# One issuing queue for all transfers of a fused attention and feed-forward kernel, in a new order

## The chip, the core and the metric

The kernel runs on one core of a Trainium2 chip. A core has a matrix engine (TensorE, PE in the rows), three engines for elementwise work (VectorE or DVE, ScalarE or ACT, GpSimd or POOL), and SyncE (SP), which here only issues transfers. Each engine works through its own list of instructions in order and waits on semaphores. Transfers (DMA) are issued from an engine's queue (SPq, ACTq) and carried out by 16 shared DMA engines. Time is device microseconds of one launch.

## What is computed

Eight batches of 128 tokens, 512 wide, go through one gated cross-attention and one gated feed-forward block, in float32:

```python
x = x + jnp.tanh(g_xattn[0]) * xattn(_layernorm(x), ctx, ctx, Wq, bq, Wk, bk, Wv, bv, Wo, bo)
x = x + jnp.tanh(g_ffn[0]) * ffn(_layernorm(x), w1, w1_scale, w3, w3_scale, w2, w2_scale)
# xattn: 32 query heads of 16 over 8 key heads, softmax(Q K^T / 4) V, then Wo
# ffn: silu(x W1^T) * (x W3^T), then W2^T; 1792 inner columns, weights scaled by 128 x 128 blocks
```

## The kernel before

**Precision.** Most products are made from a high and a low piece of each operand (three matmuls, lines 1871 to 1873): names that end in H and L, or PH and PL for the softmax numerators.

**Attention, batch by batch.** A pair of batches shares a projection of Q (four `project_q`), K and V (`project_kv32`). K and Q go out to DRAM scratch (kscr, qscr) and come back in another layout: `keys_out`, six strips of 64 KB by `keys_in` into x2HL (whose memory holds the keys until the feed-forward needs it), `queries_out`, three blocks by `queries_in` (or `queries_part` for batch 0) into Qst. `scores(n, j)` (line 1917) makes scores only for their row maxima: VectorE reduces them (MX, Mtok), TensorE turns them (`turn_max`), they become Mrow and come back as one more strip of Qst (`max_in`). `scores_t(n, g)` (line 1928) then makes the transposed scores with the maxima subtracted by that strip, together with a fixed pattern `sel` that stands as rows in x2HL (`select_rows`). ScalarE takes the exponential twice (E and PH), GpSimd makes PL = E - PH (line 460), `values(n, g)` multiplies with V (lines 1936, 1937), VectorE divides (on), and after a turn (`turn4`), aTH and aTL, `project` with the output weights WpH, WpL gives the residual (line 1279). Then the second norm: statistics, x2n, a turn, and x2H (ScalarE) and x2L (VectorE) in x2HL.

**Feed-forward.** 14 chunks of 128 inner columns in two halves of four batches. A chunk's weights arrive in wres (`weights_in`, 768 KB), GpSimd scales them (`scale`, line 471), ScalarE and VectorE split them (w13H, w13L, w2H, w2L), TensorE makes `g_or_u` and `y`. The first three chunks start among the last attention work. The first `y` waits for the last x2L, since its four banks of PSUM are those of the attention work.

**What sets the order.** Everything is one straight program per engine, written out by hand up to the loop of the feed-forward. Transfers are issued by SyncE (lines 266 to 411) and, for 22 of them, by ScalarE between its compute instructions. Buffers with few slots tie the engines together: E and PL have four slots, Qst three, the keys four batches.

The lines on which most turns: the third part of the first queries and what waits for it,

```python
            queries_part(sp, 0, 0, 0, 2, q_in1a)      # SyncE, line 297
            out_weights_in(sp)                        # 1 MB, line 298
            queries_part(act, 0, 1, 0, 2, q_in1a)     # ScalarE, line 830
            pe.wait_ge(q_in1a, 48)                    # TensorE, ahead of scores(0, 0)
```

Of the kernel before, what the change touches and what calls it, by code (L numbers as in the profile page):

```python
# [66 lines left out]
def build(nc, x, ctxt, wproj, bias, small, wff, out):  # L67
    with ExitStack() as ctx:
# [3 lines left out]
        def sem(name):  # L72
            return ctx.enter_context(nc.semaphore(name))
# [101 lines left out]
        mean2_ok, ve2_ok, rs2_ok, nb2_ok, x2n_ok, x2T_ps = (sem(n) for n in ("mean2_ok", "ve2_ok", "rs2_ok", "nb2_ok", "x2n_ok", "x2T_ps"))
        x2H_ok, x2L_ok, q_in2, q_in0, nb2_ok_pool, x2n_ok_dve = (sem(n) for n in ("x2H_ok", "x2L_ok", "q_in2", "q_in0", "nb2_ok_pool", "x2n_ok_dve"))
        scaled, w13H_ok, w13L_ok, g_ps, u_ps, t_ok = (sem(n) for n in ("scaled", "w13H_ok", "w13L_ok", "g_ps", "u_ps", "t_ok"))
        a_ok, h_ok, hH_ok, w2H_ok, w2L_ok, hL_ok = (sem(n) for n in ("a_ok", "h_ok", "hH_ok", "w2H_ok", "w2L_ok", "hL_ok"))
        y_used, warmed = sem("y_used"), sem("warmed")
# [17 lines left out]
        def select_rows(eng, b):  # L197
            done = (sel_in0, sel_in1, sel_in2, sel_in3)[b]
            eng.dma_start(r32(kst(b)[ROWS:ROWS + NM, :, :]), sel[ROWS:ROWS + NM, :, :]).then_inc(done, 16)
# [67 lines left out]
        def _(sp):  # L267
# [6 lines left out]
            for b in (2, 3):  # L274
                tokens_in(sp, b)
                context_in(sp, b)

            sp.wait_ge(kh_out, 16)
            keys_in(sp, 0, 2, 1)
            keys_in(sp, 0, 0, 1)  # L280
            sp.wait_ge(kl_out, 16)
            keys_in(sp, 0, 1, 1)
            sp.wait_ge(qT_H, 2)
            queries_out(sp, 0, 0, 0, 2, qh_outa)
            keys_in(sp, 0, 1, 0)
            keys_in(sp, 0, 2, 0)
            tokens_in(sp, 5)
            sp.wait_ge(kT_H_dve, 1)
            keys_out(sp, 1, 0)
            sp.wait_ge(kT_L, 2)  # L290
            keys_out(sp, 1, 1)
# [6 lines left out]
            out_weights_in(sp)  # L298
            sp.wait_ge(kh_out, 32)
            keys_in(sp, 1, 0, 1)  # L300
            tokens_in(sp, 6)
# [3 lines left out]
            queries_part(sp, 0, 2, 2, 4, q_in1)  # L305
            sp.wait_ge(kT_L, 3)
            keys_out(sp, 2, 1)
            keys_out(sp, 2, 0)
            keys_in(sp, 1, 1, 0)
            queries_in(sp, 1, 2, q_in2)  # L310
            queries_in(sp, 1, 0, q_in2)
            context_in(sp, 6)
            keys_in(sp, 1, 2, 1)
            context_in(sp, 7)
            sp.wait_ge(sel_ok, 3)
            select_rows(sp, 3)
            sp.wait_ge(mrows, 1)
            max_in(sp, 0, 0, 2)
            sp.wait_ge(qT_H, 8)
            queries_out(sp, 1, 0, 0, 4, qh_out)  # L320
            sp.wait_ge(qT_L, 8)
            queries_out(sp, 1, 1, 0, 4, ql_out)
            sp.wait_ge(qh_out, 32)
            queries_in(sp, 2, 0, q_in0)
            sp.wait_ge(ql_out, 32)
            queries_in(sp, 2, 2, q_in0)
            keys_in(sp, 1, 2, 0)
            keys_in(sp, 1, 1, 1)
            sp.wait_ge(kT_H_dve, 3)
            keys_out(sp, 3, 0)  # L330
            select_rows(sp, 1)
# [2254 lines left out]
```

## Time and profile before

| | before |
|---|---|
| median of 3 runs | 393.6 us (390.91 to 394.44) |
| the profiled execution | 394.24 us |
| its span in the trace | 392.5 us |
| TensorE busy | 369.7 us, 94% of the span |
| VectorE, ScalarE, GpSimd busy | 259.1, 182.3, 152.8 us |
| mean granted clock of TensorE | 0.982 of full speed |
| DMA | 34.96 MB, 89 GB/s over the span |

The profile is of one execution. A row of a timeline has a start, a duration and, in brackets, how long the engine was idle ahead of it and which instruction or transfer ended that. The time of an instruction that is blocked while it holds its engine is in its duration, not in the brackets.

### The profile page before, as it was taken

Reading aid. Unit: us, or ns where it says so; the run is one execution under the profiler, and the core shown is the slowest. Engines: PE = TensorE matmul, PEld = TensorE weight load, DVE = VectorE, ACT = ScalarE, POOL = GpSimd, SP = SyncE. Lnnn points to the kernel's source line nnn. Section 1 sums busy time; section 2 is a strip of 40 time slices with the busy share of each in tenths; the row PEclk is TensorE's granted clock in tenths of the full one; section 3 lists DMA queues with packets and bytes.
Section 4 is the critical chain, followed back from the end, with each engine's and each line's share of the span. In section 5 each row is a group of like instructions: output and inputs, shape, how many; then the busy total and the mean of one; then the engine's idle time right before and its main releaser. Section 6 shows DMA issues by size and latency. Waiting matters only on the chain.

```text
span 392.5 us, 6021 instructions
## 1 busy us (share of the span) xinstructions
PE 369.7 (94%) x2216; PEld 303.0 (77%) x2216; DVE 259.1 (66%) x417; ACT 182.3 (46%) x316; POOL 152.8 (39%) x134
## 2 busy tenths in 40 slices
PE   8977699979999999879999999999999999999996
PEld 6967589868677878658888888888888888888885
DVE  4764869969999967876776777543855344544334
ACT  3442579858889985243233242232242232332320
POOL 5463558979999987442333344000000000000000
PEclk9996989999999999989999999999999999999999
DMA  8899545936861310691000000000200000000002
GB/s 302 267 320 238 182 100 112 243 85 205 199 163 28 104 71 2 249 424 51 0 0 0 0 0 0 0 0 0 109 1 0 0 0 0 0 0 0 0 0 107
DMA packets 15604, 34.96 MB, mean 89 GB/s; under 512 B 2176, under 2 KB 7296, under 8 KB 14784
## 3 DMA queue, kind: packets, MB, share of 16 engines
q1 hardware_dynamic: 12080, 28.84, 24.0%
q10 hardware_dynamic: 3504, 5.86, 5.3%
q8 instruction: 12, 0.20, 0.2%
q14 instruction: 8, 0.07, 0.1%
HBM read 26.04 MB, written 7.34 MB: 85 GB/s over the span
## 4 chain that ended last, share of the span: by engine, by line
PE 55%; DVE 1%; issue 0%
PE ps L1871 19%; PE ps L1873 18%; PE ps L1872 18%; DVE X L1306 1%; DVE hL L1328 0%
## 5 line engine op out<-in xcount | busy, mean ns | idle before, releaser
L1871 PE MATMUL ps<-x2HL,w13H 128*128 128x512 f32 x224 | 89.0, 397 | 0.0
L1873 PE MATMUL ps<-x2HL,w13L 128*128 128x512 f32 x224 | 88.5, 395 | 0.0
L1872 PE MATMUL ps<-x2HL,w13H 128*128 128x512 f32 x224 | 88.4, 395 | 0.0
L460 POOL TENSOR_TENSOR PL<-E,PH 128x512 f16<-128x512 f32 x64 | 74.1, 1177 | 12.3 <-ACT PH L753 4.8
L471 POOL TENSOR_TENSOR wres<-wres,gsc 128x1536 f32<-128x1536 f32 x14 | 41.8, 2989 | 49.3 <-DVE hf L1319 49.3
L772 ACT ACTIVATE T<-ps 128x512 f32<-128x512 f32 x28 | 16.7, 597 | 79.4 <-PE ps L1873 79.4
L1873 PEld LDWEIGHTS ps<-x2HL,w13L 128*128 128x128 f32 x224 | 42.0, 187 | 10.4
L1872 PEld LDWEIGHTS ps<-x2HL,w13H 128*128 128x128 f32 x224 | 42.0, 188 | 10.0
L1871 PEld LDWEIGHTS ps<-x2HL,w13H 128*128 128x128 f32 x224 | 42.0, 188 | 9.6
L1312 DVE SCALAR_TENSOR_TENSOR A<-T,ps 128x512 f32<-128x512 f32 x28 | 19.2, 686 | 45.4 <-ACT T L772 45.4
L1871 PE MATMUL ps<-w2H,hH 128*128 128x512 f32 x112 | 45.1, 403 | 2.3 <-DVE x2HL L1295 2.3
L1248 DVE TENSOR_REDUCE MX<-ps 128x8 f32<-128x1024 f32 x32 | 38.9, 1217 | 12.5 <-PE ps L1917 12.1
L780 ACT ACTIVATE hH<-hf 128x512 fp32r<-128x512 f32 x28 | 17.7, 631 | 62.9 <-DVE hf L1319 62.9
L1873 PE MATMUL ps<-w2H,hL 128*128 128x512 f32 x112 | 44.3, 395 | 0.0
L1872 PE MATMUL ps<-w2L,hH 128*128 128x512 f32 x112 | 44.1, 394 | 0.0
L1319 DVE SCALAR_TENSOR_TENSOR hf<-A,ps 128x512 f32<-128x512 f32 x28 | 19.2, 687 | 32.4 <-PE ps L1873 32.1
L753 ACT ACTIVATE PH<-ps 128x512 f16<-128x512 f32 x64 | 37.2, 599 | 6.9 <-PE ps L1928 6.9
L1328 DVE TENSOR_TENSOR hL<-hf,hH 128x512 fp32r<-128x512 f32 x28 | 38.3, 1369 | 2.4
L750 ACT ACTIVATE E<-ps 128x512 f32<-128x512 f32 x64 | 37.4, 598 | 3.8 <-PE ps L1928 3.7
L1300 DVE TENSOR_TENSOR w13L<-wres,w13H 128x1024 fp32r<-128x1024 f32 x28 | 34.1, 1219 | 5.4 <-ACT w13H L767 5.4
L1928 PE MATMUL ps<-Qst,x2HL 112*128 112x512 f32 x64 | 27.5, 445 | 3.5 <-DMA Qst<-Mrow 3.5
L1917 PE MATMUL ps<-x2HL,Qst 96*128 96x256 f32 x128 | 22.6, 302 | 8.3 <-DMA Qst<-qscr 4.4
(103 smaller groups left out, 651.7 us busy)
## 6 DMA issues: line engine op xcount, KB each, us to landing
wres<-in_wff SPq DMA_DIRECT2D x12, 768.0 KB, 7.7
Qst<-qscr SPq DMA_DIRECT2D x19, 256.0 KB, 4.5
X<-in_x SPq DMA_DIRECT2D x6, 256.0 KB, 6.0
qscr<-QTH SPq DMA_DIRECT2D x3, 512.0 KB, 2.9
qscr<-QTL SPq DMA_DIRECT2D x3, 512.0 KB, 4.9
wres<-in_wff ACTq DMA_DIRECT2D x2, 768.0 KB, 7.0
out<-X SPq DMA_DIRECT2D x6, 256.0 KB, 2.1
x2HL<-kscr SPq DMA_DIRECT2D x20, 64.0 KB, 4.3
```

The lines of the kernel that those rows point to most:

```text
L460: pool.tensor_tensor(PL[:, g % NL, :], E[:, g % NE, :], PH[:, g, :], ALU.subtract).then_inc(pL_ok, 1)
L471: pool.tensor_tensor(w, w, v, ALU.mult).then_inc(scaled, 1)
L750: act.activation(E[:, g % NE, :], ps[:, g % 2, :], ACT.Exp, scale=SCALE).then_inc(E_ok, 1)
L753: act.activation(PH[:, g, :], ps[:, g % 2, :], ACT.Exp, scale=SCALE).then_inc(PH_ok, 1)
L1248: dve.tensor_reduce(MX[:, j, :, :], ps[:, b:b + 2, :].rearrange("p b (x g k) -> p (b x) g k", x=2, g=2), AX.X, ALU.max).then_inc(max_ok, 1)
L1300: dve.tensor_tensor(w13L[:, s, :], wres[:, n, 0:W13], r32(w13H[:, s, :]), ALU.subtract).then_inc(w13L_ok, 1)
L1328: dve.tensor_tensor(hL[:, s, :], hf[:, s, :], r32(hH[:, s, :]), ALU.subtract).then_inc(hL_ok, 1)
L1871: pe.matmul(out_ap, aH, bH, start=start, stop=False)
L1872: pe.matmul(out_ap, aH, bL, start=False, stop=False)
L1873: return pe.matmul(out_ap, aL, bH, start=False, stop=stop)
L1917: m = pe.matmul(ps[:, b + h // 2, (h % 2) * TWO:(h % 2 + 1) * TWO], Qst[0:ROWS, slot(n), h, j * P:(j + 1) * P], kst(n)[0:ROWS, 2 * h:2 * h ...
L1928: pe.matmul(ps[:, g % 2, :], kst(n)[0:ROWS + NM, g, :], Qst[0:ROWS + NM, slot(n), g // 2, :], start=True, stop=True).then_inc(st_ps, 1)
```

## The change

- All 22 transfers that ScalarE issued during the attention go to SyncE; ScalarE keeps its first three. SyncE's list goes from 98 to 120 transfers, in a new order: the 1 MB of output weights behind all parts of the first queries and two blocks of the next, tokens and context 6 and 7 behind those, feed-forward chunks 0 and 1 behind a group of keys and queries.
- The select pattern is made on GpSimd first of all and its four strips go out right after the first ten loads, under one semaphore.
- x2n is made on ScalarE for all eight batches (VectorE made the last one). ScalarE also takes the bias copies of V (VT) and three of K (KTH) from VectorE, VectorE takes a max strip and its low half.
- The interleaving of all engines' lists is written anew around that. The instructions of TensorE are the same, but one V projection stands earlier and one K projection later than the first scores, and two thirds of an output projection move behind the last `values`.

```diff
@@ SyncE, from the first wait on
+            sp.wait_ge(sel_ok, 3)
+            for b in range(NKST):
+                select_rows(sp, b)
+            sp.wait_ge(kT_H, 1)
+            keys_out(sp, 0, 0)
+            sp.wait_ge(kT_L, 1)
+            keys_out(sp, 0, 1)
+            sp.wait_ge(v_ps, 1)
+            context_in(sp, 4)
+            context_in(sp, 5)
+            tokens_in(sp, 4)
...
             queries_part(sp, 0, 0, 0, 2, q_in1a)
-            out_weights_in(sp)
+            queries_part(sp, 0, 1, 0, 2, q_in1a)
+            sp.wait_ge(ql_outa, 16)
+            queries_part(sp, 0, 2, 0, 2, q_in1a)
...
             queries_in(sp, 1, 0, q_in2)
+            out_weights_in(sp)
+            queries_in(sp, 1, 1, q_in2)
             context_in(sp, 6)
...
@@ VectorE
-            def normalise2(n):
-                dve.tensor_scalar(x2n[:], X[:, n, :], rs2[:, n % 2, 0:1], nb2[:, n % 2, 0:1], ALU.mult, ALU.add).then_inc(x2n_ok_dve, 1)
```

**Place 1: SyncE, from the second half of the first queries out to the first max strip.** qscr is the scratch for queries, Qst<-qscr the way back, raw<-in_wproj the output weights, x2HL<-kscr a strip of keys. Before:

```order
L223 DMA qscr<-QTL 128x2x256
L231 DMA Qst<-qscr 32x4x256
L205 DMA raw<-in_wproj 128x2048
L219 DMA x2HL<-kscr 16x4x256
L202 DMA X<-in_x 128x512
L231 DMA Qst<-qscr 32x4x256 x2
L214 DMA kscr<-KTL 128x256
L214 DMA kscr<-KTH 128x256
L219 DMA x2HL<-kscr 16x4x256
L227 DMA Qst<-qscr 32x2048 x2
```

and after the change:

```order
L221 DMA qscr<-QTL 128x2x256
L229 DMA Qst<-qscr 32x4x256 x3
L212 DMA kscr<-KTH 128x256
L229 DMA Qst<-qscr 32x4x256 x3
L225 DMA Qst<-qscr 32x2048 x2
L203 DMA raw<-in_wproj 128x2048
L225 DMA Qst<-qscr 32x2048
L240 DMA ct<-in_ctxt 128x512
L200 DMA X<-in_x 128x512
L240 DMA ct<-in_ctxt 128x512
L200 DMA X<-in_x 128x512
```

All six parts of batch 0 and two blocks of batch 1 now stand ahead of the output weights; three of the parts were ScalarE's before.

**Place 2: SyncE, the strips and blocks of the fifth batch (its third pair).** Before, with the first chunk of feed-forward weights (wres) issued by ScalarE meanwhile:

```order
L235 DMA Qst<-Mrow 16x4x512
L219 DMA x2HL<-kscr 16x4x256 x2
L227 DMA Qst<-qscr 32x2048 x3
L219 DMA x2HL<-kscr 16x4x256 x3
L235 DMA Qst<-Mrow 16x4x512
```

and after:

```order
L233 DMA Qst<-Mrow 16x4x512
L217 DMA x2HL<-kscr 16x4x256 x3
L225 DMA Qst<-qscr 32x2048
L217 DMA x2HL<-kscr 16x4x256 x2
L225 DMA Qst<-qscr 32x2048 x2
L217 DMA x2HL<-kscr 16x4x256
L237 DMA wres<-in_wff 128x1536
```

The chunk of weights now follows all nine transfers on the same queue.

**Place 3: VectorE, the end of the attention.** hf is the gated product of the feed-forward, the x2HL rows are the low pieces of the second norm. Before:

```order
L1319 SCALAR_TENSOR_TENSOR hf<-A,ps 128x512
L1252 TENSOR_SCALAR x2n<-X,rs,nb 128x512
L1324 TENSOR_TENSOR w2L<-wres,w2H 128x512
L1295 TENSOR_TENSOR x2HL<-ps,x2HL 128x4x128 x2
L1328 TENSOR_TENSOR hL<-hf,hH 128x512
L1324 TENSOR_TENSOR w2L<-wres,w2H 128x512
```

and after:

```order
L1306 TENSOR_TENSOR x2HL<-ps,x2HL 128x4x128
L1335 TENSOR_TENSOR w2L<-wres,w2H 128x512
L1330 SCALAR_TENSOR_TENSOR hf<-A,ps 128x512
L1306 TENSOR_TENSOR x2HL<-ps,x2HL 128x4x128
L1339 TENSOR_TENSOR hL<-hf,hH 128x512
L1335 TENSOR_TENSOR w2L<-wres,w2H 128x512
L1306 TENSOR_TENSOR x2HL<-ps,x2HL 128x4x128
L1339 TENSOR_TENSOR hL<-hf,hH 128x512
```

x2n is gone from VectorE, and the last x2HL has two w2L and an hL ahead of it.

## Rows read from the trace of the kernel before

**Rows 1.** The page: busy time and share of the span by engine.
```profile
PE 369.7 (94%) x2216; PEld 303.0 (77%) x2216; DVE 259.1 (66%) x417; ACT 182.3 (46%) x316; POOL 152.8 (39%) x134
```
**Rows 2.** Windows: from:to, length, then busy by engine, clock, DMA share, GB/s.
```profile
0.00:27.70 27.70, 25.37 (x138) 22.00 (x138) 17.78 (x43) 11.92 (x20) 14.75 (x21) 1.00 0.91 300
27.70:49.20 21.50, 13.65 (x89) 12.93 (x89) 12.66 (x21) 7.93 (x13) 10.17 (x10) 0.84 0.83 211
49.20:60.00 10.80, 10.80 (x86) 9.56 (x87) 7.64 (x17) 8.07 (x17) 6.52 (x7) 0.84 0.41 95
60.00:82.60 22.60, 19.75 (x213) 17.45 (x211) 19.96 (x41) 19.64 (x40) 21.17 (x24) 1.00 0.72 183
82.60:150.90 68.30, 65.93 (x682) 52.46 (x683) 58.24 (x132) 57.48 (x111) 61.73 (x58) 1.00 0.42 113
150.90:170.20 19.30, 15.19 (x83) 11.97 (x79) 17.76 (x27) 9.30 (x15) 10.61 (x7) 1.00 0.51 202
170.20:177.40 7.20, 7.20 (x25) 5.85 (x26) 4.89 (x7) 2.10 (x3) 2.76 (x1) 0.76 1.01 420
177.40:392.50 215.10, 211.83 (x913) 170.81 (x911) 120.18 (x133) 65.80 (x98) 25.11 (x8) 1.00 0.03 11
```
**Rows 3.** Timeline of TensorE: start, duration, and the idle before it.
```profile
27.40 0.28 PE L1873 MATMUL ps<-xTH,WpL 128*128 128x256 f32 x1
32.11 2.05 PE L1917 MATMUL ps<-x2HL,Qst 96*128 96x256 f32 x8 [4.43 <-DMA Qst<-qscr]
...
49.18 0.73 PE L1928 MATMUL ps<-Qst,x2HL 112*128 112x512 f32 x2 [3.18 <-DMA Qst<-Mrow]
...
82.61 0.73 PE L1917 MATMUL ps<-x2HL,Qst 96*128 96x256 f32 x4 [2.85 <-DMA x2HL<-kscr]
...
150.90 0.18 PE L1937 MATMUL ps<-Vp,PL 128*128 128x49 bf16 x1
...
165.82 0.66 PE L1879 MATMUL ps<-ident,x2n 128*128 128x128 f32 x4 [1.81 <-DVE x2n L1252]
...
170.18 0.80 PE L1871 MATMUL ps<-w2H,hH 128*128 128x512 f32 x1 [2.30 <-DVE x2HL L1295]
```
**Rows 4.** DMA issues around 22.5 us: what, size, us from issue to landing.
```profile
raw<-in_wproj SPq DMA_DIRECT2D x1, 1024.0 KB, 9.0
Qst<-qscr ACTq DMA_DIRECT2D x1, 128.0 KB, 9.7
```
**Rows 5.** Windows 17.3 to 40.8 and 1.5 to 12.5.
```profile
17.30:40.80 23.50, 18.28 (x116) 17.02 (x115) 13.92 (x30) 9.49 (x16) 9.85 (x12) 0.85 0.97 263
...
1.50:12.50 11.00, 10.99 (x46) 9.10 (x47) 6.21 (x15) 5.58 (x8) 7.15 (x8) 1.00 0.99 357
```
**Rows 6.** DMA issues around 42.9 us: the second max strip.
```profile
Qst<-Mrow ACTq DMA_DIRECT2D x1, 64.0 KB, 6.5
```
**Rows 7.** ScalarE's timeline at 74; DMA issues around 76.4 us.
```profile
74.44 0.35 ACTq L239 DMA_DIRECT2D wres<-in_wff  x1
...
x2HL<-kscr SPq DMA_DIRECT2D x1, 64.0 KB, 6.8
```
**Rows 8.** Windows around the wait at 82.6.
```profile
70.00:82.60 12.60, 9.76 (x100) 8.24 (x98) 10.12 (x21) 9.64 (x19) 12.11 (x13) 1.00 0.81 205
82.60:90.00 7.40, 7.39 (x93) 6.72 (x94) 6.04 (x11) 4.58 (x10) 4.97 (x3) 1.00 0.30 61
```
**Rows 9.** The tail: timelines of VectorE and GpSimd; groups of w2L and of ScalarE's x2n.
```profile
162.81 2.96 DVE L1252 TENSOR_SCALAR x2n<-X,rs,nb 128x512 f32<-128x512 f32 x1 [0.43 <-POOL nb L450]
165.69 3.24 DVE L1324 TENSOR_TENSOR w2L<-wres,w2H 128x512 fp32r<-128x512 f32 x1
...
162.73 5.65 POOL L471 TENSOR_TENSOR wres<-wres,gsc 128x1536 f32<-128x1536 f32 x2
...
L1324 DVE TENSOR_TENSOR w2L<-wres,w2H x28: 679/684/3240, 165.7 to 384.4; 128x512 fp32r<-128x512 f32 x28
...
L728 ACT ACTIVATE x2n<-X,nb,rs x7: 805/827/880, 104.7 to 158.6; 128x512 f32<-128x512 f32 x7
```

More of the change, by code:

```diff
@@ L846, in _ @@
+            q_high(W2, 2)
+            act.wait_ge(q_ps, 4)
+            q_high(W1, 3)
             act.wait_ge(r1_ok, 2)
             v_second(2, W0)
+            act.wait_ge(k_ps, 2)
+            act.wait_ge(kh_out, 16)
+            act.wait_ge(kl_out, 16)
+            k_high(W2)
+            act.wait_ge(xT_ps, 3)
+            normalise(3)
+            x_high(2, W1)
+            gates()
+            act.wait_ge(v_ps, 3)
+            v_bias(W0)
+            act.wait_ge(xT_ps, 4)
+            x_high(3, W2)
@@ L1386, in _ @@
[L1386 to L1391 removed]
+            dve.wait_ge(stats1, 4)
+            mean(3)
+            dve.wait_ge(qT_H, 3)
+            q_low(W2, 2)
+            dve.wait_ge(mean1, 4)
+            epsilon(3)
+            v_residue(2, W0)
+            dve.wait_ge(rs1_ok, 4)
+            shift(3)
+            dve.wait_ge(qT_H, 4)
+            q_low(W1, 3)
+            dve.wait_ge(v2_ok_act, 2)
@@ L2227, in _ @@
             scores_t(3, 0)
+            pe.wait_ge(max_ok, 18)
+            scores(4, 2)
+            pe.wait_ge(PH_ok, 24)
+            scores_t(3, 1)
             pe.wait_ge(pL_ok, 21)
@@ L2447, in _ @@
             values(6, 4)
+            project(W1, DM, aTH, aTL, O0, 3, True).then_inc(o_ps, 1)
+            pe.wait_ge(PH_ok, 56)
+            scores_t(7, 1)
+            pe.wait_ge(PH_ok, 57)
+            scores_t(7, 2)
             pe.wait_ge(pL_ok, 54)
             values(6, 5)
-            pe.wait_ge(E_ok, 56)
-            scores_t(7, 1)
-            g_or_u(0, 0, 0, 0, range(2, KB))
+            pe.wait_ge(w13L_ok, 1)
+            g_or_u(0, 0, 0, 0, range(2))
+            pe.wait_ge(E_ok, 58)
+            scores_t(7, 3)
             pe.wait_ge(pL_ok, 55)
@@ L2487, in _ @@
             values(7, 4)
-            project(W1, DM, aTH, aTL, O0, 2)
             pe.wait_ge(pL_ok, 62)
             values(7, 5)
-            project(W1, DM, aTH, aTL, O0, 3, True).then_inc(o_ps, 1)
-            pe.wait_ge(E_ok, 63)
-            pe.wait_ge(w13L_ok, 2)
-            g_or_u(1, 1, 0, 0, range(2))
+            pe.wait_ge(x2n_ok, 5)
+            turn4(W0, x2n).then_inc(x2T_ps, 1)
+            pe.wait_ge(aTL_ok, 7)
+            project(W2, DM, aTH, aTL, O0, 0)
+            project(W2, DM, aTH, aTL, O0, 1)
             pe.wait_ge(pL_ok, 63)
```

1619 lines of the change are left out of this document (778 added, 841 removed).

## The prediction

> **What bounds the kernel now.** Start with the busy line of the page [rows 1]: TensorE is busy for 369.7 us, 94% of the span, and the next engine for 66%. So only three things can pay: TensorE's idle time (22.8 us in all), the stretches in which it ran at the lower of its two clock levels (1.2 instead of 2.4 GHz; the mean granted clock of a window tells the share), and work taken off it. The change takes no matmul away: both programs issue the same matmuls, in another order. The windows by stage [rows 2] show where the loss sits: 0 to 49.2 us holds 10.2 us of idle (2.3 + 7.9) and clock 0.84 in its second part; 49.2 to 60 is busy all through at clock 0.84; 60 to 150.9 holds 5.2 us; 150.9 to 170.2 holds 4.1, and the 7.2 us after it run at clock 0.76; from 177.4 on nothing is left but 3.3 us at the end. The waits on TensorE's own timeline [rows 3] name them: 4.43 us for Qst<-qscr before the first scores, 3.18 for the max rows before the first transposed scores (which I call ST), 2.85 for keys at 82.6, 1.81 for a normalised row block (x2n) that VectorE made, and 2.30 for x2HL before the first product with w2.
>
> **Part 1, the way to the first scores.** Scores(0,0) starts at 32.11, when the third part of the queries lands: ScalarE had issued it 9.7 us before it landed, and 1 MB of output weights, issued on SyncE's queue half a microsecond earlier, took 9.0 us beside it [rows 4]. TensorE had run dry at 27.68 [rows 3]. The change sends these parts before the 1 MB. I count the bytes that the one queue carries from the end of the first ten loads (about 12.5 us, with the DMA engines 99% busy until then [rows 5]) to that third part: four select strips 256 KB, first keys out 256, three blocks of tokens or context 768, six key strips 384, tokens 5 256, gates 85, bias 256, queries out 1024, three parts 384. Together 3669 KB, or 3.76 MB. In 17.3 to 40.8 us the DMA engines were 97% busy and moved 263 GB/s [rows 5]: 14.3 us, so 26.8. TensorE's own work ahead of it shrinks by one key projection (1.7 us), but its second query product now waits for the third V split: by the durations of ScalarE and VectorE I place it at 27.3. Scores(0,0) at 27.3 instead of 32.1.
>
> **Part 2, from there to the first ST.** Before, this took 17.1 us (32.11 to 49.18): the second max strip needed 6.5 us on ScalarE's queue, beside 1 MB of queries out on SyncE's [rows 6], so it was issued at 42.7. TensorE has exactly the same matmuls behind it at this point in both programs (three K, four V, eight query products, six score groups), so the two times compare directly. After: from the third part to the second max strip the queue carries keys out 128 KB, parts 384, queries of batch 1 768, output weights 1024, four input blocks 1024, keys 64, strip 64, keys out 128, queries out 512, strip 64: 4160 KB, 4.26 MB. All at 263 GB/s gives 16.2 us and 43.0; the 2.1 MB of wide loads at the 357 GB/s of the first loads [rows 5] and the rest at 263 gives 14.1 and 40.9. TensorE's own work reaches ST at about 41. I take 42.0 for ST, bounds 41 and 43 (45 if the V chain slips as well): gain 7.2 us, bounds 4 to 8.
>
> **Part 3, the clock behind it.** The 10.8 us from 49.2 to 60 ran at 0.84 after the 3.18 us wait: 10.8 x 0.16 = 1.7 us. The wait before ST should now be under 1 us, and after the 2.85 us wait at 82.6 the clock stayed at 1.00 [rows 3, 8]. I take the 1.7 whole; the other bound is 0.
>
> **Part 4, keys for the fifth batch.** The last of six key strips took 6.8 us to land, next to 768 KB of feed-forward weights that ScalarE had sent at 74.44 [rows 7]. Now the weights go out after all keys and queries. Those nine transfers take 384 + 768 KB, 1.18 MB, 4.5 us at 263 GB/s against issues of some 6 us, and ten us of matmuls stand between their release and their use, so the 2.85 us wait should go. But GpSimd was busy for 12.1 of the 12.6 us around it and for 5.0 of the 7.4 after it [rows 8]; it was behind and used the wait. I take half, 1.4 us, bounds 0 and 2.85. ScalarE is rid of 22 issues (0.35 us for the one in [rows 7], longer for strips) and takes seven K and V copies; busy for 57.5 of 68.3 us and 19.6 of 22.6 [rows 2] it has the room, so I put nothing down.
>
> **Part 5, the tail.** From the last value matmuls (150.90) to the first w2 product (170.18) are 19.3 us [rows 3]. VectorE's x2n took 2.96 us and w2L after it 3.24 (median 0.68), both while GpSimd ran two weight scalings in 5.65 us; ScalarE makes an x2n in 0.83 [rows 9]. So x2n goes to ScalarE and its 1.81 us wait goes. But w2L, h and w2L again now stand on VectorE ahead of the last x2L (the second order piece), for which the w2 product waits, and GpSimd's scalings are released in the same microseconds as before. Walking the queues with those durations (on 2.1 us, o_ps 7.8, x2n ready 11.5, w2L 13.9, second hf 14.6, h 17.9, w2L 18.5, x2L 19.1) gives 19.1 us, 18.3 where VectorE gets ahead of the first scaling. In addition 1.0 us of matmuls moved behind the start of this stretch. Gain 1.0 + 0.2 to 1.0; I take 1.3. The lower clock after it (0.76 for 7.2 us) I leave as it is. If nothing were blocked, x2L would be ready at 15.1 and TensorE would not wait: 3.3 us more, and 1.7 of clock.
> The Trainium skill, SBUF — State Buffer, section SBUF: two separate sides, says that VectorE and GpSimd share one port pair as an exclusive lock: whoever starts first holds it for its whole instruction, also against a VectorE instruction with two SBUF inputs. The trace agrees (2.96 and 3.24 us). By it moving x2n alone does not free the tail, which is what I forecast; without it the sum would be some 5 us lower.
>
> **The sum.** 7.2 + 1.7 + 1.4 + 1.3 = 11.6 us. The profiled execution took 394.24 us (span 392.5 [rows 1] and 1.7 around it), the median of the three runs is 393.6; the gain is in waits that every run has, so I take it from the median: 382.0.
>
> **Rivals.**
> Given back (22%): ST comes 7 us sooner, but the dense middle is held by GpSimd (61.7 of 68.3 us busy, 21.2 of 22.6 before that [rows 2]) and by ScalarE, and a strip that is now queued behind 1 MB of queries out (the fifth batch's) comes late. Then parts 3 and 4 bring nothing and two waits like the old 2.85 come in: 393.6 - 7.2 - 1.3 + 2 to 7 us, 387 to 392.
> Slower (10%): one queue moves less than two. The strip must be there by 49.2, so 6549 KB between 17.3 and 49.2: below 210 GB/s part 2 turns into a loss, and below some 180 GB/s (38 us, ST at 55) it eats everything else: 396 or more. For it: 60 to 82.6 moved only 183 GB/s [rows 2]. Against it: the DMA engines were 72% busy there, and the first loads, nearly all on SyncE's queue, made 357.
> The Trainium skill, DMA: Bandwidth & Descriptors, section Issuing engines are not separate DMA queues, says that transfers of all queues run on the same 16 engines and that issuing from several saves only issue time; by it this rival falls away. ScalarE's own queue did not let the 64 KB strip past in this trace (6.5 us), which agrees.
> More (12%): the tail is unblocked too, 382.0 - 5 = 377 or less.
> My own case 56%, 378 to 387.
>
> **Numbers.** A difference of under about 1% cannot be told from no change here (390.91 to 394.44 in three runs). Faster by over 1% is below 389.7: 56 + 12 + 14 of the 22 = 82%. Within 1%: 8 + 3 = 11%. Slower: 7%. The range 376 to 390 leaves out some 2 in 10: the slower rival, the end of "given back", and the far end of "more".
>
> **What would show it.** Right: scores(0,0) at 26 to 29 us; ST at 40 to 44 with a wait under 1.5; clock 1.00 from 30 to 60; no wait for kscr near 74; no VectorE x2n; w2L still near 3 us beside a scaling, and some 3 us of wait for x2HL before the first w2 product. Wrong: DMA busy at 97% with far less than 263 GB/s; waits for Mrow strips or keys that the trace of before does not have; GpSimd with no idle from 45 to 140 while TensorE waits for PL.

## The result, and the profile after

The changed kernel takes 390.48 us (median of 20 runs, 386.82 to 395.74), the kernel before 393.6 us (20 runs, 390.07 to 396.92). The ratio is 0.992, with a 95% interval of 0.989 to 0.995: 3.1 us less, small but clear of the noise over 20 runs, and under the 1% that the prediction could not tell from no change. Predicted were 382.0 us, 376 to 390. Of the 11.6 us forecast, 8.5 did not come. A second profile of the changed kernel, taken later, reads like the first (391.55 us); the first is shown here.

TensorE's share on the page has grown by one point, in a span that is 3.2 us shorter:

```profile
span 389.3 us, 6031 instructions
...
PE 371.2 (95%) x2216; PEld 303.8 (78%) x2216; DVE 253.6 (65%) x411; ACT 184.7 (47%) x322; POOL 154.9 (40%) x134
```

Windows of the changed kernel (columns as in [rows 2]: length; busy time of PE, PEld, DVE, ACT, POOL; granted clock, DMA share, GB/s):

```profile
0.00:27.70 27.70, 24.35 (x131) 20.68 (x132) 15.90 (x40) 14.18 (x26) 13.98 (x22) 1.00 0.85 260
27.70:49.20 21.50, 16.38 (x93) 14.96 (x91) 10.65 (x18) 6.53 (x10) 10.70 (x8) 0.76 0.91 251
49.20:60.00 10.80, 10.80 (x100) 9.82 (x99) 9.40 (x21) 9.69 (x20) 7.48 (x9) 1.00 0.56 110
```

Its TensorE timeline, the places that answer to [rows 3] (start, duration, idle before it and its releaser); L1912 are scores, L1925 transposed scores, L1893 K and V projections (x4 or x8 is the number of matmuls in a row):

```profile
29.82 1.40 PE L1912 MATMUL ps<-x2HL,Qst 96*128 96x256 f32 x8 [1.75 <-DMA Qst<-qscr]
42.02 1.19 PE L1912 MATMUL ps<-x2HL,Qst 96*128 96x256 f32 x4 [3.38 <-DMA Qst<-qscr]
43.22 2.02 PE L1893 MATMUL ps<-ct,raw 128*128 128x256 f32 x4
...
49.42 1.03 PE L1893 MATMUL ps<-ct,raw 128*128 128x256 f32 x4
50.09 0.59 PE L1925 MATMUL ps<-Qst,x2HL 112*128 112x512 f32 x1
...
80.40 0.73 PE L1912 MATMUL ps<-x2HL,Qst 96*128 96x256 f32 x4 [1.07 <-DMA x2HL<-kscr]
105.97 0.62 PE L1912 MATMUL ps<-x2HL,Qst 96*128 96x256 f32 x3 [1.62 <-DMA x2HL<-kscr]
148.13 0.18 PE L1934 MATMUL ps<-Vp,PL 128*128 128x49 bf16 x1
166.94 0.64 PE L1866 MATMUL ps<-w2H,hH 128*128 128x512 f32 x1 [2.74 <-DVE x2HL L1306]
```

Set against [rows 3], these rows divide the 3.2 us of span among the stages:

| stage | before | after | gain | predicted |
|---|---|---|---|---|
| start to first transposed scores (ST) | 49.18 | 50.09 | -0.9 | 7.2 |
| ST to last value product | 101.7 | 98.0 | 3.7 | 4.1 (parts 3 and 4, and the 1.0 of part 5 that moves behind this stage) |
| last value product to first w2 product | 19.3 | 18.8 | 0.5 | 0.3 (the rest of part 5) |
| first w2 product to end of span | 222.3 | 222.4 | -0.1 | 0 |

So everything behind ST went about as forecast, and the whole miss is ahead of it. Scores(0,0) came at 29.8 instead of 27.3. Then a wait appeared that the prediction had nowhere: 3.38 us at 42.02, before scores(1,0), for the last third of the second batch's queries (queries_in(1, 1)). Behind it the clock is at its lower level (1.2 GHz): four matmuls of a projection take 2.02 us at 43.22, and 1.03 us at 49.42. When TensorE reaches ST, it does not wait at all.

The issues of SyncE's queue at that place (its timeline: start, time to issue):

```profile
29.50 1.05 SPq L225 DMA_DIRECT2D Qst<-qscr  x2
30.59 0.42 SPq L203 DMA_DIRECT2D raw<-in_wproj  x1
31.06 0.43 SPq L225 DMA_DIRECT2D Qst<-qscr  x1
...
38.31 0.60 SPq L233 DMA_DIRECT2D Qst<-Mrow  x1
...
43.90 0.60 SPq L233 DMA_DIRECT2D Qst<-Mrow  x1
```

and what the DMA view of the changed kernel says of the 1 MB and of the queries behind it (size, us from issue to landing):

```profile
raw<-in_wproj SPq DMA_DIRECT2D x1, 1024.0 KB, 10.1
...
Qst<-qscr SPq DMA_DIRECT2D x1, 256.0 KB, 10.8
```

The change put "large loads where nothing urgent follows", but directly behind the 1 MB of output weights stands a transfer that TensorE needs at 38.6 us. It was issued at 31.06 and landed at 41.9. It also held up the second max strip, which SyncE could not issue before 43.9, since the turn of the row maxima comes behind scores(1,0) on TensorE.

### The profile page after: what moved, and what is told of

Read it like the earlier page. It is cut to its first block, busy times and chain, and to the rows that moved or that the text cites. A ratio compares the mean times of both kernels' runs of the same rounds, so it can differ in the third digit from the quotient of the medians.

```text
span 389.3 us, 6031 instructions
## 1 busy us (share of the span) xinstructions
PE 371.2 (95%) x2216; PEld 303.8 (78%) x2216; DVE 253.6 (65%) x411; ACT 184.7 (47%) x322; POOL 154.9 (40%) x134
## 4 chain that ended last, share of the span: by engine, by line
PE 56%; DVE 1%; issue 0%
PE ps L1866 19%; PE ps L1868 19%; PE ps L1867 18%; DVE X L1317 1%; DVE hL L1339 0%
## 5 line engine op out<-in xcount | busy, mean ns | idle before, releaser
L781 ACT ACTIVATE E<-ps 128x512 f32<-128x512 f32 x64 | 38.3, 604 | 2.3 <-PE ps L1925 2.3
L1912 PE MATMUL ps<-x2HL,Qst 96*128 96x256 f32 x128 | 22.5, 301 | 7.9 <-DMA Qst<-qscr 5.1
L798 ACT ACTIVATE w13H<-wres 128x1024 fp32r (+1 forms) x28 | 29.4, 1050 | 0.0
```

Source lines behind the costliest of these rows:

```text
L781: act.activation(E[:, g % NE, :], ps[:, g % 2, :], ACT.Exp, scale=SCALE).then_inc(E_ok, 1)
L798: act.activation(w13H[:, s, :], wres[:, n, 0:W13], ACT.Copy).then_inc(w13H_ok, 1)
L1912: m = pe.matmul(ps[:, b + h // 2, (h % 2) * TWO:(h % 2 + 1) * TWO], Qst[0:ROWS, slot(n), h, j * P:(j + 1) * P], kst(n)[0:ROWS, 2 * h:2 * h ...
```

## The experiments

All times are medians of five rounds against the kernel before on the same chip, unless said otherwise; the changed kernel is 390.48 us, ratio 0.992. In the diffs, - and + are against the changed kernel (e4: against the kernel before).

### e1: the third ahead of the 1 MB

```diff
+            queries_in(sp, 1, 1, q_in2)
             out_weights_in(sp)
-            queries_in(sp, 1, 1, q_in2)
```

> The changed kernel with one pair of transfers swapped: the last third of the second batch's queries (queries_in(1, 1)) goes out ahead of the 1 MB of output weights. In the changed kernel TensorE waits 3.38 us for it before scores(1,0) at 42.0, and its clock is 0.76 from 27.7 to 49.2. Theory A (only the order is wrong: what is needed next stands behind 1 MB): that third lands at 35 to 37, scores(1,0) starts at 38.6 without a wait, the first transposed scores (ST) at 45 to 47 instead of 50.1, and the kernel takes 3 to 5 us less than the changed one, 386 to 388. Theory B (the queue carries 4.26 MB up to the second max strip, and whatever stands behind the 1 MB pays): the wait moves to the split of the output weights on ScalarE, to xTL, or to the max strip, ST stays at 48 to 50, time within 1.5 us of the changed kernel's 390.5.

388.19 us, ratio 0.983 (0.977 to 0.989). The wait before scores(1,0) is gone (it starts at 39.2, and the clock is 1.00 in 27.7 to 49.2), but what stands behind the 1 MB pays in its turn. TensorE's timeline of e1:

```profile
44.24 1.10 PE L1893 MATMUL ps<-ct,raw 128*128 128x256 f32 x4 [1.49 <-DMA ct<-in_ctxt]
...
46.95 0.72 PE L1925 MATMUL ps<-Qst,x2HL 112*128 112x512 f32 x2 [0.30 <-DMA Qst<-Mrow]
```

The second max strip was issued at 40.6, 3.3 us sooner, and took 6.3 us instead of 2.7. ST at 46.95, and at 47.5 in e5, which has the same order; four profiles with the order of the changed kernel (after, its second profile, e3, e9) have it at 48.9 to 50.8. Both theories hold a part: the order costs some 2 to 3 us, the bytes the rest. In time, e1 and the changed kernel (0.977 to 0.989 against 0.989 to 0.995) are only just apart.

### e12: the third on the other queue

```diff
-            queries_in(sp, 1, 1, q_in2)
...
             act.wait_ge(q_ps, 5)
+            act.wait_ge(qh_outa, 16)
             act.wait_ge(qh_out, 16)
             act.wait_ge(ql_out, 16)
+            queries_in(act, 1, 1, q_in2)
             q_high(W1, 0)
```

> The changed kernel with queries_in(1, 1) at its time (31 to 33 us) but on ScalarE's queue instead of SyncE's, where it stood directly behind the 1 MB and took 10.8 us. If a transfer of another queue passes the 1 MB: it lands 3 to 5 us after its issue, at 36 to 37, no wait before scores(1,0), 2 to 3 us less than the changed kernel, as e1 (388.2). If the 16 engines take the two queues' work in turns but the 1 MB still fills them (kernel before: parts on ScalarE's queue took 7.2 to 9.7 us beside it): it lands at 40 to 42, scores(1,0) waits 2 to 3.5 us, time within 1 us of 390.5. The predicted 'slower' rival (one queue moves less than two) would show in more GB/s here than the 251 of the changed kernel in 27.7 to 49.2.

388.98 us, ratio 0.992 (0.989 to 0.995). The DMA view of e12:

```profile
Qst<-qscr ACTq DMA_DIRECT2D x1, 256.0 KB, 8.6
```

Issued at 31.4, 1.0 us behind the 1 MB (which landed at 39.6), it landed at 40.0: scores(1,0) waits 1.97 us instead of 3.38. On a queue of its own it did not pass the large transfer; it only lost less behind it. In this profile ST came at 47.1, as early as in e1. The Trainium skill, DMA: Bandwidth & Descriptors, section Issuing engines are not separate DMA queues, says that transfers started from any engine run interleaved on the same 16 DMA engines; the trace agrees, with these 8.6 us.

### e14: the 1 MB out of the stretch

```diff
             tokens_in(sp, 4)
+            out_weights_in(sp)
             sp.wait_ge(kl_out, 16)
...
-            out_weights_in(sp)
             queries_in(sp, 1, 1, q_in2)
```

> The changed kernel with the 1 MB of output weights moved and nothing else: issued at about 14 us, behind tokens_in(4), where SyncE idles 3 us for the keys' write, instead of at 30.6. The DMA engines were 71% busy in 17 to 29.5 us, so 29% of 12.5 us, 3.6 us, is free for it; it needs about 4. If the 1 MB in 30 to 47 us is the cause: no wait before scores(1,0), both max strips land 3 to 4 us after issue, ST at 43.5 to 45.5 instead of 50.1, clock above 0.9 in 27.7 to 49.2, 3.5 to 5 us less than the changed kernel: 385.5 to 387. If the front is as tight: scores(0,0) slips from 29.8 to 33 or more and half of it goes: 388 to 390.

This is the prediction's own step, with the 1 MB removed from it, and in the profile ST comes where the prediction had it. TensorE's timeline of e14, and one of its windows:

```profile
29.04 0.59 PE L1912 MATMUL ps<-x2HL,Qst 96*128 96x256 f32 x3 [1.71 <-DMA Qst<-qscr]
...
37.70 0.64 PE L1912 MATMUL ps<-x2HL,Qst 96*128 96x256 f32 x4
...
42.97 0.82 PE L1925 MATMUL ps<-Qst,x2HL 112*128 112x512 f32 x2
```

```profile
27.70:49.20 21.50, 20.16 (x146) 18.93 (x147) 15.89 (x28) 12.29 (x22) 14.37 (x13) 0.92 0.91 236
```

No wait before scores(1,0) nor before ST; the second max strip took 3.6 us. Of the 7.1 us, 6.6 are still there at the first w2 product (160.3 instead of 166.9) and 6.9 at the end (span 382.4 instead of 389.3). But the median of the twelve timed runs is 389.54, ratio 0.992 (0.988 to 0.997), no better than the changed kernel. The profiled execution, 384.2 us, was the fastest of them, so it is not a typical one.

> e14 again, for a profile of a usual execution (389.5 us, clock 0.982). If the front is what varies (select strips and 1 MB ahead of the first keys), the scores(0,0) or ST come 3 us or more later than 29.0 and 43.0. If the front stands as it is (ST at 43 to 45), the loss is in stretches at the lower clock level behind the waits at 74, 99 and 160 us, whose length varies: 5 us of time is 5 us less of full-speed time, 0.013 of the mean clock.

> The same kernel a third time, with the same two readings: either ST is late, or the lower clock covers more of the time behind the key waits and the 2.7 us wait before the first w2 product.

These two profiles took 385.49 and 388.23 us. In both, scores(1,0) and ST again have no wait: what follows scores(0,0) is as in the first. What varies is the front: at 14 to 17 us TensorE waits for a context block, under 0.3 us in the first profile, 2.79 and 2.98 us in these, so that scores(0,0) starts at 29.0, 32.3 and 33.2 and ST at 43.0, 44.8 and 45.8. What a timed run of e14 at 389 us looks like, none of the three shows; that stays open. So the profiles show that the 1 MB held up ST; that taking it out shortens a usual execution, this run does not show.

The same edit also tests the rival "one queue moves less than two". In e14 the one queue carries the 1 MB in the stretch ahead of scores(0,0) as well:

```profile
17.00:29.50 12.50, 9.58 (x65) 8.43 (x64) 7.81 (x20) 7.10 (x14) 4.17 (x5) 1.00 0.98 293
```

The changed kernel moved 221 GB/s in the same window, with the DMA engines 71% busy; the kernel before, with two engines issuing and its 1 MB in that stretch, moved 298. One queue can do what two did, if it has large transfers to carry.

### e3: the scalings held (the tail)

```diff
             for c in range(3, NCH):
                 need(pool, h_ok, c - 2)
+                if c == 3:
+                    pool.wait_ge(x2L_ok, NBATCH)
+                if c == 4:
+                    pool.wait_ge(w13L_ok, 4)
                 scale(c)
```

> The changed kernel with GpSimd's scaling of chunk 3 held until VectorE's last x2L, and of chunk 4 until w13L of chunk 3; nothing is left out. If VectorE's 3.24 us for w2L is a wait for GpSimd's 5.9 us of scalings (instead of 0.68 alone), w2L takes 0.68, x2L is ready at about 163.8 to 164.4, the first w2 product starts at 164 to 164.5 instead of 166.94 without a wait, the lower clock behind it (3.4 us of matmuls at half speed) goes too: 2.5 to 4.2 us less than the changed kernel, 386.3 to 388. Rival: VectorE's 3.24 us has another cause (the operation itself): no change. Second rival: the scalings, later now, come late for chunk 3: TensorE waits 1 to 2 us before the gate products of chunk 3 and half of the gain goes.

387.49 us, ratio 0.983 (0.978 to 0.988). VectorE in the changed kernel, and behind it GpSimd's two scalings beside it:

```profile
163.04 3.24 DVE L1335 TENSOR_TENSOR w2L<-wres,w2H 128x512 fp32r<-128x512 f32 x1
166.21 0.68 DVE L1306 TENSOR_TENSOR x2HL<-ps,x2HL 128x512 fp32r<-128x512 f32 x1
...
159.82 5.92 POOL L494 TENSOR_TENSOR wres<-wres,gsc 128x1536 f32<-128x1536 f32 x2
```

and the same in e3, with the later scalings of the same kernel and the two VectorE instructions beside them:

```profile
161.34 0.69 DVE L1339 TENSOR_TENSOR w2L<-wres,w2H 128x512 fp32r<-128x512 f32 x1
161.94 0.68 DVE L1310 TENSOR_TENSOR x2HL<-ps,x2HL 128x512 fp32r<-128x512 f32 x1
...
169.71 2.15 DVE L1339 TENSOR_TENSOR w2L<-wres,w2H 128x512 fp32r<-128x512 f32 x1
171.78 3.25 DVE L1343 TENSOR_TENSOR hL<-hf,hH 128x512 fp32r<-128x512 f32 x1
...
162.76 3.08 POOL L494 TENSOR_TENSOR wres<-wres,gsc 128x1536 f32<-128x1536 f32 x1 [4.00 <-issue]
168.54 5.93 POOL L494 TENSOR_TENSOR wres<-wres,gsc 128x1536 f32<-128x1536 f32 x2 [2.70 <-issue]
...
162.95 0.39 PE L1870 MATMUL ps<-w2H,hH 128*128 128x512 f32 x1
```

w2L takes 0.69 instead of 3.24 us, and the first w2 product needs no wait: from the last value product it is 15.9 us instead of 18.8. That is so in every profile: 15.9 in the eight kernels with this edit, 18.8 in the ten profiles of the changed kernel and its variants without it. The scalings stretch w2L and hL when they run later, by 4 us together, but there TensorE has work in store and waits only 0.75 us at 175. The 3.24 us is shown to be a wait for GpSimd, not the operation. The Trainium skill, SBUF — State Buffer, section SBUF: two separate sides, tells of the port pair that VectorE and GpSimd lock against each other; these rows agree with it.

### e5 and e17: the edits together

> The two edits that each took time off, together: queries_in(1, 1) ahead of the 1 MB, and GpSimd's scalings of chunks 3 and 4 held. Alone they took 388.19 and 387.49 us against 390.48 of the changed kernel. They work 100 us apart, so the gains should add: 2.3 + 3.0, 385.2 us (384.5 to 386.5); about 387.5 if one eats the other.

385.05 us, ratio 0.980 (0.973 to 0.988): as expected to 0.2 us. The interval is too wide to show that the gains add: it holds the ratio of e1 or e3 alone (0.983) as well as their sum (0.974).

> The changed kernel with the 1 MB at 14 us (e14) and GpSimd's scalings held (e3). Alone: 389.54 and 387.49 us against 390.48. If the medians add: 389.54 - 3.0 = 386.5. If e14's profile (384.15, ST at 43.0, no wait before scores(1,0)) is what the edit gives and its median was lowered by the clock alone, this profile shows ST at 43 to 45 again, and the time is 381 to 384. If the early ST is not kept in a usual execution, this profile shows ST at 46 or later or a wait (max strip, context, keys) that e14's does not have.

383.98 us, ratio 0.976 (0.970 to 0.983), ST at 44.3 without a wait, span 380.5. Against e3 alone (387.49) the early 1 MB is worth 3.5 us here, against 0.9 alone (e14); the intervals of e3 and e17 overlap, so the 3.5 us are not shown.

### e2 and e4: the 1 MB later

e2 moves out_weights_in behind the second max strip, e4 does the change's own move (behind queries_in(1, 0)) in the kernel before. Both put ScalarE's split of the weights behind x_high(5):

```diff
             x_high(5, W1)
+            weights_high(wo_in, O0, PW, woH_ok)
```

> The changed kernel with the 1 MB of output weights moved behind the second max strip of the first batch, and ScalarE's split of them moved behind x_high(5). Theory A and B both expect no wait before scores(1,0) and ST at 43.5 to 45 (TensorE has 5.0 us of matmuls between scores(1,0) at 38.6 and ST), clock above 0.9 from 27.7 to 49.2. They part behind it: if the whole gain of ST (5 to 6 us) is carried on, the kernel takes 384 to 386; if GpSimd's low part of these weights (4.5 us), now at about 47 to 52 and ahead of its first PL, becomes the bound (rival 'given back' of the prediction), TensorE waits for PL before values(0,0) and the time is 388 to 390.

> The kernel before with one part of the change alone: the 1 MB of output weights goes out behind queries_in(1, 0), and ScalarE's split of them behind x_high(5). By the prediction's part 1 this MB is what the third part of the first queries waits for: scores(0,0) starts at 27.7 to 29 instead of 32.1. If that is carried to ST (49.2 in the kernel before) and on, the kernel takes 389 to 391, 3 to 4 us less than before. Rival (given back at the max strip and the next queries, which stand behind the same MB in their turn): ST at 47.5 or later and the time within 1.5 us of the kernel before.

e2: 394.02 us, ratio 1.004 (1.000 to 1.008). ST started at 43.5, as expected, and was then paid for: ScalarE stood in front of the late weights with the V copy behind it. e4: 399.04 us, ratio 1.011 (1.007 to 1.016), slower although scores(0,0) started at 29.2 instead of 32.1: a context block behind the 1 MB came late, and GpSimd, 4.5 us on the weights' low part, was late with PL. The profiled execution of e4 is its fastest (394.3 us); the other five took 396.6 to 399.8, and what they lost beyond these two waits no profile shows. TensorE's timeline of e2, and of e4:

```profile
50.03 0.80 PE L1893 MATMUL ps<-ct,raw 128*128 128x256 f32 x1 [5.22 <-ACT VT L766]
```

```profile
41.86 1.19 PE L1898 MATMUL ps<-ct,raw 128*128 128x256 f32 x2 [3.52 <-DMA ct<-in_ctxt]
...
54.45 0.20 PE L1936 MATMUL ps<-Vp,PH 128*128 128x49 bf16 x1 [2.60 <-POOL PL L460]
```

The weights have a date of their own on ScalarE and GpSimd. My place for the split in e2 was a poor one, so e2 does not tell what a better place would give.

### e8 and e10: the select strips later

e8 moves the four select strips behind the first batch's query parts (changed kernel, nothing else). e10 is e5 with the strips behind the context blocks 6 and 7.

> The changed kernel with one part undone: the four select strips (256 KB) go out behind the first batch's query parts instead of ahead of the first keys. The prediction counted them at 1.0 us of the way to scores(0,0) (29.8 in the changed kernel, 27.3 predicted); the trace also shows context blocks 2 and 3 landing behind them, with TensorE waiting 0.86 to 2.4 us. If they cost what they weigh: scores(0,0) about 1 us sooner, at 28.5 to 29; since queries_in(1, 1) then still stands behind the 1 MB and these strips, the wait before scores(1,0) grows by as much and the time stays within 0.7 us of 390.5. If the first wait was theirs and its microsecond is carried: 389.5 or less.

390.59 us, ratio 0.996 (0.992 to 1.000): the same as the changed kernel. TensorE's timeline of e8:

```profile
27.84 1.17 PE L1911 MATMUL ps<-x2HL,Qst 96*128 96x256 f32 x8 [0.32 <-DMA Qst<-qscr]
...
40.02 0.77 PE L1911 MATMUL ps<-x2HL,Qst 96*128 96x256 f32 x2 [3.96 <-DMA Qst<-qscr]
...
48.21 0.59 PE L1924 MATMUL ps<-Qst,x2HL 112*128 112x512 f32 x1
```

Scores(0,0), scores(1,0) and ST all come 2 us sooner than in the changed kernel; the wait for the third behind the 1 MB grows by only 0.6 us. The 2 us are lost behind ST: the last value product is at 148.07, against 148.13. TensorE waits 1.87 us for a key strip at 79.3, instead of 1.07 at 80.4, and the mean clock from ST to the last value product is 0.98 instead of 1.00.

Why scores(0,0) moved, SyncE's queue shows. Changed kernel, and e8:

```profile
13.38 0.43 SPq L200 DMA_DIRECT2D X<-in_x  x1
16.37 1.21 SPq L217 DMA_DIRECT2D x2HL<-kscr  x2
```

```profile
13.44 0.43 SPq L200 DMA_DIRECT2D X<-in_x  x1
13.91 1.30 SPq L217 DMA_DIRECT2D x2HL<-kscr  x2
```

In the changed kernel SyncE stood still from 13.8 to 16.4 us, until the low piece of the first keys had landed in scratch: 5.2 us after its issue, with the four select strips ahead of it. In e8 it landed in 2.8 us and nothing stood still.

> e5 with the four select strips moved from ahead of the first keys to behind the context blocks 6 and 7. In e8 they left scores(0,0) at 27.8 instead of 29.8 to 32.5 (six profiles with them in front), but scores(1,0) then waited 3.96 us for queries_in(1, 1) behind the 1 MB. Here that third is ahead of the 1 MB. If the two causes are separate and each is worth what its wait shows: scores(0,0) at 27.8, scores(1,0) at 35 to 36 without a wait, ST at 44.5 to 46 (47.5 in e5), all bytes being the same; time 1.5 to 3 us less than e5's 385.05: 382 to 383.5. Rival: up to ST the same bytes must cross anyway, so the wait moves to the context blocks or the max strip (ST at 47 or later) and the time stays within 1 us of 385.

386.44 us, ratio 0.983 (0.978 to 0.988), no better than e5. Scores(0,0) at 28.5 and scores(1,0) at 37.2 without a wait, as the first theory had it, but ST at 45.8:

```profile
45.79 0.77 PE L1928 MATMUL ps<-Qst,x2HL 112*128 112x512 f32 x2 [2.98 <-DMA Qst<-Mrow]
```

The max strip took 6.4 us behind the same bytes. ST is where the first theory had it (44.5 to 46), and 1.7 us sooner than in e5, but the wait moved to the max strip, as the rival said, and the time is neither theory's. What ST gained was lost behind it: from ST to the last value product e10 takes 101.5 us and e5 97.6, with longer waits for key strips (1.59 and 2.19 us against 0.95 and 1.33) and a mean clock of 0.97 against 1.00.

### e6, e11, e13, e15: further orders

e6 is e5 with the token blocks 6 and 7 and a key strip behind the max strips; e11 is e10 with the context blocks ahead of the 1 MB and the split behind x_high(4); e13 is e10 with the 1 MB at 14 us; e15 is e13 with the keys of e9.

> e5 with the token blocks 6 and 7 and one key strip (576 KB) moved behind the second max strip. In e1 that strip took 6.3 us to land (40.63 to 46.9), behind everything issued since 33, and TensorE waited 1.49 us for a context block behind the 1 MB. Theory A (bytes ahead in the queue decide): 0.59 MB at 286 GB/s is 2.1 us, the strip lands at 44.5 to 45, the context blocks 0.9 us sooner, ST at 45 to 46 instead of 47.0, time 1 to 2 us less than e5. Rival: what is moved is then late itself (statistics(6) on VectorE, ahead of k_low and x_low, the next keys): no gain or a loss of 1 us.

387.78 us, ratio 0.986 (0.980 to 0.992), against 385.05 of e5. ST at 46.2 instead of 47.5, but the key strip moved is late itself (1.89 us before scores at 55.5): the rival, at 2.7 us where it said up to 1.

> e10 with the context blocks 6 and 7 (512 KB) ahead of the 1 MB of output weights, and ScalarE's split of these weights behind x_high(4) instead of ahead of it. In e1 and e5 TensorE waited 1.3 to 1.5 us at 44.3 for a context block behind the 1 MB. If that wait still stands in e10, this takes it: 0.5 to 1.5 us less than e10. Rival, as in e4 (PL late by 2.60 us): output weights 1.8 us later hold ScalarE (x_high(5), k_high) and GpSimd (low part, 4.5 us, then PL): 0 to 2 us more than e10.

384.71 us, ratio 0.980 (0.975 to 0.984); not to be told from e10 or e5. The context wait went, and TensorE waited 3.50 us at 43.9 for a row block that ScalarE made behind the late weights.

> e10 with the 1 MB of output weights issued at about 14 us, behind tokens_in(4). In e10 ST waited 2.98 us for the second max strip (issued 39.35, landed 45.8, 6.4 us behind about 2 MB), and the clock behind it fell. Without the 1 MB in that stretch the strip should take 3 us and land at 42.5 to 43; TensorE has 5 us of matmuls behind scores(1,0) at 36 to 37, so ST at 42 to 44 with under 1 us of wait and the clock at 1.00: 2.5 to 4 us less than e10's 386.4, 382.5 to 384. Rival: the 1 MB delays keys and queries in front of scores(0,0) (28.5 in e10) by 2 us or more, and ScalarE's 1.9 us and GpSimd's 4.5 us on it, released earlier, stand in front of V and statistics: time within 1 us of e10 or e5 (385).

383.89 us, ratio 0.976 (0.970 to 0.983). Scores(0,0) slipped to 30.5, ST at 46.1 with 0.55 us of wait; better than e10 by 2.5 us.

> e13 (383.9 us) with three of the six key strips of batches 4 and 5, and of 6 and 7, issued by ScalarE (as e9). In e13 TensorE waits 2.01 us at 77.1 and 1.40 at 102.5 for the last key strip; in e9 the two waits were 0.88 and 0.59 against 1.07 and 1.62. If they are worth their length: 1 to 2 us less than e13, 382 to 383. If GpSimd or the clock gives it back, as e9 (0.4 us): 383.5.

383.53 us, ratio 0.973 (0.968 to 0.979), the fastest kernel of the study by a margin that its interval does not carry: e13, e15 and e17 are one result, 9.3 to 10.1 us below the kernel before.

### e9: the keys' waits

Three of six key strips, for batches 4 and 5 and again for 6 and 7, go out on ScalarE's queue.

> The changed kernel with three of the six key strips of batches 4 and 5, and three of those of 6 and 7, issued by ScalarE instead of SyncE. In the changed kernel TensorE waits 1.07 us at 80.4 and 1.62 at 106.0 for the last of them, while the DMA engines are 76% and 64% busy and nine issues stand 0.6 to 0.7 us apart: theory C, the issues of one engine are the limit there, not the bytes. Then the last strip lands 1.5 to 2 us sooner and both waits go. By the prediction's part 4 GpSimd gives half of it back: 1.2 to 1.5 us less than the changed kernel, 389.0 to 389.3; all of it, 2.7 us, if GpSimd was not the bound; nothing if the strips take as long on two queues (bytes or row count decide).

390.07 us, ratio 0.993 (0.990 to 0.997): no change to be told. The waits at 80.7 and 105.2 are 0.88 and 0.59 instead of 1.07 and 1.62, and a new one of 0.60 us for queries stands at 115. The last strips landed at 80.6 and 105.2 instead of 80.4 and 105.9: theory C falls for the first group and holds for 0.7 us in the second.

### The changed kernel again

> The changed kernel, unchanged, for a second profile. Six kernels with the same front had scores(0,0) at 29.3 to 32.5 us and the changed kernel at 29.8, so I expect 29.8 to 32.5 here; scores(1,0) waits for queries_in(1, 1) by 1.5 to 3.5 us, ST at 49 to 51, and the first w2 product waits 2.7 us for x2HL, as that is fixed by the order of the instructions.

391.55 us: scores(0,0) at 30.6, scores(1,0) at 42.5 after 3.05 us of wait, ST at 50.8, clock 0.76 in 27.7 to 49.2, 2.74 us before the first w2 product. The reading of the first profile stands.

## Why the prediction was wrong, point by point

**Part 1, scores(0,0) at 27.3: 29.8 (30.6 in the second profile).** The bytes were counted and divided by 263 GB/s, as if the queue were never empty. Two things were left out. The first is seen in e8: SyncE stood still for 2.6 us at 13.8, waiting for the first keys to land behind the select strips; with the strips moved the stand is gone and scores(0,0) comes at 27.8, 2.0 of the 2.5 us (28.5 and 29.0 in e10 and e11, which move them too). The edit takes the strips' own 256 KB out as well, 1.0 us by the prediction's sum, so it does not give the stand a price of its own. The second: from 16.37 to 29.46 us SyncE never rests, but 20 transfers of mostly 64 to 256 KB leave 0.65 us apart; the third part was issued only at 26.35, and the sum had it landed by 26.8. The windows, of the kernel before (with its 1 MB in the stretch) and of the changed one:

```profile
17.30:32.10 14.80, 9.59 (x61) 8.33 (x60) 8.02 (x21) 5.90 (x11) 9.04 (x11) 0.94 1.04 298
```

```profile
17.00:29.50 12.50, 10.10 (x69) 8.91 (x68) 8.04 (x22) 7.47 (x15) 4.00 (x6) 1.00 0.71 221
```

The DMA engines were 71% busy and moved 221 GB/s where they had moved 298. It looks like the rival "one queue moves less than two", which got 10%, but the queue is not the limit: in e14 it moved 293 GB/s in this same window, with the 1 MB added, and scores(0,0) came no later for it in that profile (29.04). What the sum lacked is the time to issue many small transfers, and the stand ahead of them. The 357 GB/s with which the rival was argued away was no fair test either: those first loads are 256 or 512 KB each and wide, these 64 to 256 KB and mostly strips. The rule from the Trainium skill with which the prediction set this rival aside (DMA: Bandwidth & Descriptors, section Issuing engines are not separate DMA queues) goes on to say that several issuers save only the issue time, "usually small relative to the DMA itself"; here, at 0.65 us for transfers that the engines, at 263 GB/s, move in 0.25 to 1 us, it was not small.

**Part 2, ST at 42.0: 50.1.** This is the step that failed. It summed all bytes up to the second max strip and compared the sum with TensorE's total work up to ST ("TensorE's own work reaches ST at about 41"). But TensorE consumes in order, and scores(1,0) has a transfer of its own to wait for, which stood directly behind the 1 MB. Walked with the prediction's own rate there is no room: three thirds of queries and the 1 MB, 1.83 MB behind the last part (landed at 32.0), at 263 GB/s are 7.0 us, 39.0, against TensorE's need at 38.6. It came at 41.9, since transfers issued behind it were carried beside it: the engines moved 247 GB/s in between, 2.4 MB, so by this estimate 0.6 MB of later ones. The wait of 3.38 us, its clock loss and the late max strip behind it follow from that. The rate was a second error: 4.26 MB from 29.7 (last of the first three parts landed) to 46.6 (second strip landed) are 252 GB/s, not the 302 that the mixed estimate came to; the 357 taken for the wide loads was not reached: 35.4 to 44.5 us, when they land, moved 276. The runs take the step apart: the order alone (e1, e5) moves ST to 47.0 and 47.5; the 1 MB taken out of the stretch (e14) to 43.0 to 45.8 in three profiles. Counted from scores(0,0), which leaves part 1 out, the prediction had 14.7 us to ST; the changed kernel took 20.3 and 20.2 in its two profiles, e1 and e5 15.4 and 15.1, e14 13.9, 12.5 and 12.6. So 5.6 of the 8.1 us by which ST was late belong to this step. Two more profiles with the changed kernel's order (e3, e9) took 17.2 and 18.3: the better order takes back some 2 to 5 us, the 1 MB out of the stretch all of it.

**Part 3, the clock in 49.2 to 60: right at its place, given back ahead of it.** The clock there is 1.00, worth the 1.7 us. But in 27.7 to 49.2 it fell to 0.76 where it had been 0.84 [rows 2]: 0.08 of 21.5 us, 1.7 us again. The two profiles have the same mean clock, 0.982: the wait moved, and its clock loss with it.

**Part 4, the keys: 1.4 predicted.** The wait of 2.85 us fell to 1.07, a gain of 1.8. A wait of the same kind grew at 106 us, to 1.62 (0.61 at 108.2 in the kernel before). Net 0.8. The stage from ST to the last value product gained 3.7 us, of which 1.0 is the matmuls that moved behind its end; that leaves 2.7 for parts 3 and 4, against 3.1. GpSimd did not take it back, as the other half of the estimate had feared.

**Part 5, the tail: 1.3 predicted, 0.5 from the last value product on.** All that was said of the mechanism held: no x2n on VectorE, w2L at 3.24 us beside a scaling, 2.74 us of wait for x2HL (about 3 predicted). The walk through the queues gave 19.1 us for the stretch; it took 18.8. e3 confirms the lock and what was said to lie beyond it: 2.9 us less in the stretch (3.3 predicted), and 3.0 in the time.

**The rivals.** "Given back" (22%, 387 to 392) has the right time, but not its mechanism: ST did not come sooner to begin with. "Slower" (one queue moves less than two) did not happen: its point of decision was 210 GB/s between 17.3 and 49.2 us, and there the one queue moved 240, against 248 with two before:

```profile
17.30:49.20 31.90, 23.23 (x150) 21.23 (x148) 20.22 (x40) 13.23 (x23) 15.34 (x16) 0.89 0.90 248
```

```profile
17.30:49.20 31.90, 25.80 (x156) 23.40 (x154) 17.98 (x37) 13.35 (x24) 12.78 (x12) 0.84 0.84 240
```

The bytes came nearly as fast as before; they came in an order in which TensorE could not use them.

## What to carry over

Before summing bytes to a milestone, walk the queue transfer by transfer and write beside each one when its first reader needs it: a large transfer is harmless only if the reader of everything behind it can wait for its duration (10 us here), and in e12 another queue did not get past it. Where small transfers (here 64 to 256 KB) follow each other, count issues too, and the waits of the issuing engine: one engine at 0.65 us each left the DMA engines idle for 29% of the time, and e14 put 1 MB there without a later scores(0,0) in its first profile (29.0; 32.3 and 33.2 in the others). A gain has to be read from the end of the next stages, not from the wait that went: e8 and e10 each brought ST some 2 us sooner than the kernel they change and had lost it by the last value product.

## What was not expected of the hardware

The scatter between executions goes with the granted clock. Over the 85 timed executions of the kernel before beside these experiments (389.1 to 398.1 us), time and mean granted clock have a correlation of -0.87, and 0.01 of clock goes with 3.5 us. Which of the two causes the other it does not say: in the profiles the lower level stands mostly at and behind waits. The kernels differ in it too: the mean over the executions of e4 is 0.978, over those of e5 0.993. The front scatters too: the wait for a context block at 14 to 17 us was 0.86 and 1.90 us in the two profiles of the changed kernel and 0.25 to 2.98 in those of e14. From one profile alone a gain is read too large or too small by some us.

A 64 KB strip of keys or maxima took 2.6 to 4.8 us in the changed kernel from issue to landing nearly everywhere, and 6.6 and 9.9 us for the two that were issued at 38.3 and 34.8, while the 1 MB and the blocks behind it were on their way; the time shows in no engine's row until somebody waits for it.
